# A quarter of the hypernetwork sums moves from TensorE's delta units to GpSimd

## The chip, the cores and the metric

The kernel runs on one core of a Trainium2 chip. The metric is the device time of one launch in microseconds. The five engines of the core run their own instruction streams and meet only at semaphores: TensorE (PE: matmuls, and transposes written as matmuls with an identity), VectorE (DVE), ScalarE (ACT), GpSimd (POOL), and SyncE (SP), which here issues the DMAs.

## The reference, cut to what matters

Two layers, one after the other, over x of shape 4 x 1024 x 512.

```python
# layer 0: a gated block with quantised down projection
scale = cond @ norm_w.T + 1.0
h = x * (scale[:, None, :] * rsqrt(mean(x * x) + EPS))
val, gate = split(h @ up_w.T, 2)             # 2 x 2048 columns
h = val * gelu(gate)
y = act_quant(h) @ weight_quant(down_w).T    # a scale for each row of h
x = y + x
# layer 1: an adapter whose weights depend on the batch
dWd = ((cond @ Wdd.T + bdd) * 0.1).reshape(B, 128, 512)   # Wdd: 65536 x 128
dWu = ((cond @ Wdu.T + bdu) * 0.1).reshape(B, 512, 128)   # Wdu: 65536 x 128
down = relu(einsum('bld,bnd->bln', x, Wd + dWd) + bd)
out = x + einsum('bln,bdn->bld', down, Wu + dWu) + bu
```

The change concerns `cond @ Wdd.T` and `cond @ Wdu.T`: four conditions of 128 numbers against 131,072 rows of 128 numbers, 64 MB of weights. They are called the deltas.

## The kernel before, in words

**Chunks and slots.** The 4096 rows of x are done in 8 chunks of 512 (`c` = 0 to 7). In each, layer 0 makes 16 tiles of h, one for each slot `j` (0 to 15) of the loop `run`. In slot j TensorE makes the gate product (12 matmuls of 512 columns into one of two GATE banks), then the value product (12 more into one of two VAL banks). ScalarE applies gelu to the gate; VectorE multiplies value, descale and gelu into h[j] (L925); ScalarE takes the absolute value of h[j] (L643), and VectorE, in the next slot, folds that into a running maximum (L839). After slot 15 the maximum is turned, gives a scale for each row, and in slots 0 to 7 of the next chunk VectorE multiplies the sixteen tiles of h by the scales (`quantise`, L812), with ScalarE rounding them. In slots 9 to 12 TensorE makes the down products of the chunk before, 16 matmuls each (`down_products`, L1188), and VectorE adds the residual one slot later (`residual`, L882).

**Waits that matter.** TensorE's gate product of slot n waits for gelu n-2, its value product for h n-2 (`pe.wait_ge(h_done, n - 1)`); a down product waits for the residual before it.

**Delta units.** The rows of Wdd and Wdu are cut into 128 units. For a unit SP loads two halves of 256 KB (`load_nat`, L352; a ring of three) and VectorE transposes each by 32 x 32 blocks (`turn_nat`, L829). After each eight units TensorE multiplies two batches of four units by the conditions (`delta_products`, L1147, 32 instructions for a batch, four column tiles of the array side by side). ScalarE copies the bank to `stage` (`read_sums`, L616), and SP stores it in DRAM (L356). The functions `units_at` and `batch_at` say in which slot that is.

**The end of the deltas.** In slot 6 of the last chunk SP reads all deltas back in the layout of the layers (`load_deltas`, L363 and L366). In slots 10 to 13 TensorE turns them, one batch of x a slot (`turn_deltas`, L1159 down, L1164 up), and in the following slot VectorE adds them to the base weights (`layer_of_batch`, L845 and L854). Then layer 1 runs over the eight chunks (the last 75 us).

**GpSimd** makes one small power for each chunk (`norm_x`, L509) and, at the end, adds bu to the rows (L534). Each engine carries out its program strictly in order; no scheduler is at work.

Of the kernel before, what the change touches and what calls it, by code (L numbers as in the profile page):

```python
# [15 lines left out]
P = 128  # L16
# [9 lines left out]
def conditioned_block(nc, x, cond, norm_w, up_w, down_w, Wd, bd, Wu, bu, Wdd, bdd, Wdu, bdu, out):  # L26
# [11 lines left out]
    GROUPS = 16  # L38
    UNITS, HALVES, NATT = 128, 3, 8
# [6 lines left out]
    delta_of = delta_dram.rearrange("g (t q b) (y k m) -> y b (g t) k q m", t=4, q=8, b=NB, y=2, k=2)  # L46
# [4 lines left out]
    with ExitStack() as ctx:  # L51
# [61 lines left out]
        with (nc.sbuf_tensor("delta_reg", [P, 2 * NATT + HALVES, 512], F32) as delta_reg,  # L113
              nc.sbuf_tensor("w_hi", [P, KD, 2 * FF], F16) as w_hi,
              nc.sbuf_tensor("w_lo", [P, KD, 2 * FF], F16) as w_lo):
            pass
# [15 lines left out]
        nat = delta_reg[:, 2 * NATT:, :]  # L132
# [11 lines left out]
        FIRST_SLOT, PAIRS = 3, 4  # L144

        def pieces(i):
            o = 2 * (FIRST_SLOT + i % PAIRS)
# [32 lines left out]
        def first_bank(c, k):  # L180
# [11 lines left out]
        nat_in = [sem(f"nat_in{t}") for t in range(HALVES)]  # L192
        upn_in = [sem(f"upn_in{i}") for i in range(3)]
# [17 lines left out]
        absrun_turned, max_read, scale_step, s_turned, s_bc_done = (sem(n) for n in (  # L211
            "absrun_turned", "max_read", "scale_step", "s_turned", "s_bc_done"))
# [69 lines left out]

        def units_at(c, j):
            if is_first(c):
                return [j - 13] if j >= 13 else []
            if c == NCH - 1:
                return [UNITS - 5 + j] if j < 5 else []
            u = 3 + 20 * (c - 1) + j + min(max(j - 9, 0), 4)
            return [u, u + 1] if 9 <= j < 13 else [u]

        def batch_at(c, j):
            before = units_at(c, j - 1) if j > 0 else units_at(c - 1, FT - 1) if c > 0 else []
            return [m for u in before if u % NATT == NATT - 1 for m in (u // 4 - 1, u // 4)]
# [7 lines left out]
        def _(sp):  # L301
# [44 lines left out]
            def load_nat(v):  # L346
                u, k = v // 2, v % 2
                m, t = u // 4, u % 4
                src = (Wdd, Wdu)[m % 2].rearrange("(a u p e) h -> u p a (e h)", a=2, p=P, e=4)[4 * (m // 2) + t, :, k, :]
# [8 lines left out]
            def load_deltas():  # L358
                sp.wait_ge(stage_free, 16 * (GROUPS + 1))
                sp.wait_ge(nat_turned, 2 * UNITS)  # L360
                for b in range(NB):
                    for k in range(2):
                        sp.dma_start(delta_d[64 * k:64 * k + 64, b, :], delta_of[0, b, :, k, 0:4, :]).then_inc(delta_back, 16)  # L363
                    for k in range(KD):
                        part = delta_of[1, b, 32 * (k % 2):32 * (k % 2) + 32, k // 2, 0:4, :]
# [1062 lines left out]
```

## Time and profile before

| | |
|---|---|
| time, median of 3 runs | 944.22 us (943.78 to 944.37) |
| time of the profiled execution | 944.56 us, its span 942.8 us |
| busy: PE, PEld, DVE, ACT, POOL | 934.1, 463.7, 675.2, 437.8, 53.3 us |
| granted TensorE clock | 0.999 of full speed |
| HBM | 112.72 MB read, 20.97 MB written |

Busy time is the time in which at least one instruction of the engine was under way. Matmuls are pipelined, so PE busy 99% of the span says that it was hardly ever without work, not that it worked at its peak. Times of the trace are counted from the span's start; what lies between the span and the execution's own time is 1.8 us.

### The profile page before, as it was taken

What the parts mean: (1) busy time and instruction counts of PE and PEld (TensorE: products, weight loads), DVE (VectorE), ACT (ScalarE), POOL (GpSimd) and SP (SyncE); (2) the same over time, 40 slices, a digit from 0 to 9 for tenths busy, and PEclk for the clock granted to TensorE, in tenths of its full rate; (3) what the DMA queues carried; (4) which work ended last, traced back from release to release, by engine and by line L of the source; (5) the groups of instructions that cost most, each with busy time, mean ns of one, the idle gap of its engine ahead of it and who ended that gap; (6) DMA issues with size and microseconds to landing.
All of it is one profiled execution on the core that took longest, in us unless ns stands there. A gap on an engine that the chain in (4) does not pass through costs nothing.

```text
span 942.8 us, 13789 instructions
## 1 busy us (share of the span) xinstructions
PE 934.1 (99%) x5266; PEld 463.7 (49%) x5266; DVE 675.2 (72%) x1030; ACT 437.8 (46%) x800; POOL 53.3 (6%) x53
## 2 busy tenths in 40 slices
PE   9999999999999999999999999999999999999998
PEld 6555544444444444444444444444444444445586
DVE  6778788767877596767877687767876684256766
ACT  7898677224731276214742166214642155114443
POOL 1000000000000000000000000000000000000564
PEclk9999999999999999999999999999999999999999
DMA  8899654564346543665347543555447434321584
GB/s 299 234 219 207 169 151 130 151 193 136 101 140 173 158 134 112 162 165 159 107 136 172 158 136 99 173 168 145 118 128 179 147 92 141 103 71 31 185 306 179
DMA packets 118810, 145.36 MB, mean 154 GB/s; under 512 B 51796, under 2 KB 57432, under 8 KB 118232
## 3 DMA queue, kind: packets, MB, share of 16 engines
q1 hardware_dynamic: 118744, 144.48, 53.7%
q8 instruction: 41, 0.67, 0.3%
q14 instruction: 25, 0.20, 0.1%
HBM read 112.72 MB, written 20.97 MB: 142 GB/s over the span
## 4 chain that ended last, share of the span: by engine, by line
PE 92%; DVE 3%; ACT 2%; issue 1%; DMA 1%; SPq 0%; POOL 0%; DVEq 0%; POOLq 0%; ACTq 0%
PE bank L1088 22%; PE bank L1089 22%; PE bank L1090 22%; PE bank L1188 10%; PE bank L1147 6%; PE bank L1198 1%; PE bank L1345 1%; PE bank L1323 1%; PE bank L1332 1%; DVE delta_reg L829 1%; PE bank L1068 1%; PE bank L1353 1%; PE bank L1355 1%; PE bank L1354 1%; PE bank L1362 1%
## 5 line engine op out<-in xcount | busy, mean ns | idle before, releaser
L1088 PE MATMUL bank<-x_split,w_hi 128*128 128x512 f16 x1016 | 385.3, 379 | 0.0
L1090 PE MATMUL bank<-x_split,w_lo 128*128 128x512 f16 x1016 | 385.2, 379 | 0.0
L1089 PE MATMUL bank<-x_split,w_hi 128*128 128x512 f16 x1016 | 385.2, 379 | 0.0
L829 DVE STREAM_TRANSPOSE delta_reg<-delta_reg 128x512 f32<-128x512 f32 x256 | 262.1, 1106 | 51.5 <-DMA delta_reg<-in_L_cond_Wdu 19.1
L643 ACT ACTIVATE g<-h 128x512 f32<-128x512 f32 x128 | 80.6, 630 | 304.8 <-DVE h L925 304.8
L1090 PEld LDWEIGHTS bank<-x_split,w_lo 128*128 128x128 f16 x1016 | 99.3, 98 | 119.8
L1088 PEld LDWEIGHTS bank<-x_split,w_hi 128*128 128x128 f16 x1016 | 99.4, 98 | 119.5 <-issue 6.6
L1089 PEld LDWEIGHTS bank<-x_split,w_hi 128*128 128x128 f16 x1016 | 99.4, 98 | 113.3
L925 DVE SCALAR_TENSOR_TENSOR h<-bank,desc,g 128x512 f32<-128x512 f32 x128 | 93.0, 727 | 83.6 <-issue 57.4
L627 ACT ACTIVATE g<-bank,desc 128x512 f32<-128x512 f32 x128 | 87.5, 684 | 115.8 <-PE bank L1090 115.3
L1188 PE MATMUL bank<-wqT,qreg 128*128 128x512 fp8e4 x448 | 101.3, 379 | 0.0
L839 DVE TENSOR_TENSOR absrun<-absrun,g 128x512 f32<-128x512 f32 x120 | 82.5, 687 | 24.5 <-ACT g L643 23.7
L812 DVE TENSOR_TENSOR h<-h,s_bc 128x512 f32<-128x512 f32 x112 | 71.7, 681 | 1.7 <-ACT s_bc L605 1.7
L1188 PEld LDWEIGHTS bank<-wqT,qreg 128*128 128x128 bf16 x448 | 43.8, 98 | 52.9
L598 ACT ACTIVATE h<-h 128x512 f32<-128x512 f32 x112 | 64.5, 622 | 9.2 <-DVE h L812 9.2
L601 ACT ACTIVATE qreg<-h 128x512 bf16<-128x512 f32 x112 | 63.6, 617 | 0.0
L1147 PE MATMUL bank<-delta_reg,cond_diag 128*32 128x256 f32 x1024 | 58.8, 381 | 0.1
L882 DVE SCALAR_TENSOR_TENSOR xr<-bank,fy,xr 128x512 f32<-128x512 f32 x30 | 22.4, 750 | 46.1 <-DMA xr<-in_x 20.3
L509 POOL TENSOR_TENSOR rstd<-ss,mhalf 128x4 f32<-128x4 f32 x7 | 9.7, 1379 | 666.0 <-DVE ss L776 666.0
L1147 PEld LDWEIGHTS bank<-delta_reg,cond_diag 128*32 128x32 f32 x1024 | 31.6, 110 | 26.4 <-issue 6.8
L573 ACT ACTIVATE xr<-qreg 128x512 f32<-128x512 f32 x32 | 20.1, 629 | 3.7 <-DMA qreg<-in_L_cond_up_w 3.1
L534 POOL TENSOR_TENSOR out_own<-xn,sc_row 128x512 f32<-128x512 f32 x8 | 10.0, 1288 | 195.8 <-DVE h L1032 193.3
(175 smaller groups left out, 628.0 us busy)
## 6 DMA issues: line engine op xcount, KB each, us to landing
delta_reg<-in_L_cond_Wdd SPq DMA_DIRECT2D x128, 256.0 KB, 2.9
delta_reg<-in_L_cond_Wdu SPq DMA_DIRECT2D x128, 256.0 KB, 2.9
qreg<-in_L_cond_up_w SPq DMA_DIRECT2D x32, 256.0 KB, 4.8
xr<-in_x SPq DMA_DIRECT2D x30, 256.0 KB, 3.7
x_scratch<-xr SPq DMA_DIRECT2D x30, 256.0 KB, 3.2
xn<-in_x SPq DMA_DIRECT2D x7, 1024.0 KB, 6.0
h<-in_L_cond_down_w SPq DMA_DIRECT2D x4, 1024.0 KB, 7.5
delta_reg<-in_L_cond_down_w SPq DMA_DIRECT2D x8, 512.0 KB, 4.8
```

The lines of the kernel that those rows point to most:

```text
L598: act.activation(h[:, k, :], h[:, k, :], ACT.Copy, bias=ROUND).then_inc(round_added, 1)
L627: act.activation(g[:, j % 2, :], GATE[j % 2][:, :], ACT.Gelu, scale=desc[:, 2 * j + 1:2 * j + 2]).then_inc(gelu_done, 1)
L643: act.activation(g[:, j % 2, :], h[:, j, :], ACT.Abs).then_inc(abs_done, 1)
L812: dve.tensor_tensor(h[:, k, :], h[:, k, :], s_bc[:, :], ALU.mult).then_inc(h_scaled, 1)
L829: dve.transpose(natT[:, t, k, :, :].rearrange("p a (r e) -> p e a r", e=4), nat[:, v % HALVES, :]).then_inc(nat_turned, 1)
L839: dve.tensor_tensor(absrun[:, :], absrun[:, :], g[:, j % 2, :], ALU.max).then_inc(max_done, 1)
L925: dve.scalar_tensor_tensor(h[:, j, :], VAL[j % 2][:, :], desc[:, 2 * j:2 * j + 1], g[:, j % 2, :], ALU.mult, ALU.mult).then_inc(h_done, 1)
L1088: pe.matmul(bank[:, :], w_hi[:, k, cols], xh[:, par, k, :], start=(k == 0), stop=False)
L1089: pe.matmul(bank[:, :], w_hi[:, k, cols], xl[:, par, k, :], start=False, stop=False)
L1090: mm = pe.matmul(bank[:, :], w_lo[:, k, cols], xh[:, par, k, :], start=False, stop=(k == KD - 1))
L1147: mm = pe.matmul(HY[32 * t:32 * t + 32, cols], cond_diag[:, a, :], natT[:, (4 * m + t) % NATT, :, a, :], start=(a == 0), stop=(a == HB - 1))
L1188: mm = pe.matmul(Y[:, :], q[:, f, t * P:(t + 1) * P], wqT[:, f, :], start=(f == 0), stop=(f == FT - 1))
```

## The change

- `UNITS` falls from 128 to 96: all of Wdd, and the half of Wdu that makes rows 0 to 127 and 256 to 383 of dWu. A batch is four units, `NATT` (the ring of transposed units) falls from 8 to 4, so that a batch must be multiplied before the next unit is transposed. A table `unit_slots` gives the slots, with one left out after each batch. TensorE's batches come singly.
- The other half of Wdu is 64 parts. For each, SP loads 256 KB as it lies (`load_part`, 512 runs of 512 bytes, a ring of three). GpSimd multiplies it by each of the four conditions (`multiply_part`: 4 products of 128x512), adds upper and lower half of the 128 columns (2 sums of 512 results), then again (2 sums of 256 results). VectorE sums the 32 that are left (`sum_part`, one reduction from 512 to 16 in each partition) and so has these columns of dWu in place without a turn. Parts have fixed slots in VectorE's order: 5, 7, 9, 10, 11, 12, 13, 15 of chunk 1; 1, 3, 5, 7, 9, 10, 11, 12, 13, 15 of chunks 2 to 6; 1, 3, 5, 7, 9, 10 of chunk 7.
- `s_bc` now holds the four conditions in all partitions, and VectorE's `quantise` reads the scales from the bank TB itself; ScalarE's copy of them is gone. `layer_of_batch` uses `stage` in place of `s_bc`.
- The turn of the up deltas is 2 transposes for a batch of x in place of 4, and stands behind the value product of its slot (`turn_delta_up`). The deltas come back by 32 DMAs in place of 24.

```diff
-    UNITS, HALVES, NATT = 128, 3, 8
+    UNITS, HALVES, NATT = 96, 3, 4
+    PARTS = 64
...
+        for n in range(FT * NCH):
+            long_slot = n >= FT and 9 <= n % FT < 13
+            while free_from <= n and sum(map(len, unit_slots.values())) < UNITS and len(unit_slots.get(n, [])) < 1 + long_slot:
+                u = sum(map(len, unit_slots.values()))
+                unit_slots.setdefault(n, []).append(u)
+                if u % NATT == NATT - 1:
+                    free_from = n + 2
...
+            def load_part(i):
+                if i >= 3:
+                    sp.wait_ge(part_step, 8 * (i - 3) + 6)
+                d = 128 + 4 * i + 128 * (i // 32)
+                sp.dma_start(part_w[:, i % 3, :, :], Wdu.rearrange("(d n) h -> n d h", n=BN)[:, d:d + 4, :]).then_inc(part_in[i % 3], 16)
...
+                    i = part_at(FT * c + j)
+                    if i is not None and 1 <= i < PARTS - 2:
+                        load_part(i + 2)
...
+            def multiply_part(i):
+                pool.wait_ge(part_in[i % 3], 16 * (i // 3 + 1))
+                for pair in range(2):
+                    if i > 0 or pair > 0:
+                        pool.wait_ge(part_step, 8 * i + 4 * pair)
+                    for b in range(2):
+                        pool.tensor_tensor(part_mul[:, b, :, :], part_w[:, i % 3, :, :],
+                                           cond_all[:, 2 * pair + b, :].unsqueeze(1).to_broadcast([P, 4, C]), ALU.mult).then_inc(part_step, 1)
+                    pool.wait_ge(part_step, 8 * i + 4 * pair + 2)
+                    pool.tensor_tensor(part_mul[:, :, :, 0:64], part_mul[:, :, :, 0:64], part_mul[:, :, :, 64:128], ALU.add).then_inc(part_step, 1)
+                    pool.wait_ge(part_step, 8 * i + 4 * pair + 3)
+                    if i > 0 and pair == 0:
+                        pool.wait_ge(part_summed, i)
+                    pool.tensor_tensor(part_low[:, 2 * pair:2 * pair + 2, :, :], part_mul[:, :, :, 0:32], part_mul[:, :, :, 32:64],
+                                       ALU.add).then_inc(part_step, 1)
...
-                    dve.wait_ge(s_bc_done, c + 1)
+                    dve.wait_ge(s_turned, c + 1)
...
-                    dve.tensor_tensor(h[:, k, :], h[:, k, :], s_bc[:, :], ALU.mult).then_inc(h_scaled, 1)
+                    dve.tensor_tensor(h[:, k, :], h[:, k, :], TB[:, :], ALU.mult).then_inc(h_scaled, 1)
...
+            def sum_part(i):
+                dve.wait_ge(part_step, 8 * i + 8)
+                dve.tensor_reduce(part_sum[:, :, 4 * i:4 * i + 4], part_low, AX.X, ALU.add).then_inc(part_summed, 1)
...
+            def turn_delta_up(b):
                 if b > 0:
                     pe.wait_ge(layers_ready, 2 * b)
-                for k in range(KD):
+                for k in range(0, KD, 2):
                     mm = pe.transpose(TB[:, k * P:(k + 1) * P], delta_u[:, k, b, :], identf[:, :])
                 mm.then_inc(delta_turned, 1)
```

Two places of the order show what moves. The first is SP's queue in slots 5 to 8 of the last chunk. Before, after the last loads of Wdu come the last store of `stage` (delta_scratch<-stage), the 24 loads of `load_deltas` (delta_reg<-delta_scratch), bu, and the residual's rows (xr<-in_x):

```order
L356 DMA delta_scratch<-stage 128x512
L363 DMA delta_reg<-delta_scratch 64x4x128 x2
L366 DMA delta_reg<-delta_scratch 128x1x128 x4
...
L363 DMA delta_reg<-delta_scratch 64x4x128 x2
L366 DMA delta_reg<-delta_scratch 128x1x128 x4
L446 DMA sc_row<-in_L_cond_bu 128x512
L371 DMA xr<-in_x 128x512 x2
```

Now L399 is `load_part`; the row of it above the store loads part 62, the one below bu loads part 63, the last:

```order
L399 DMA delta_reg<-in_L_cond_Wdu 128x4x128
L381 DMA delta_scratch<-stage 128x512
L389 DMA delta_reg<-delta_scratch 32x4x128
L392 DMA delta_reg<-delta_scratch 16x4x128 x2
L393 DMA delta_reg<-delta_scratch 128x1x128
...
L392 DMA delta_reg<-delta_scratch 16x4x128 x2
L393 DMA delta_reg<-delta_scratch 128x1x128
L488 DMA sc_row<-in_L_cond_bu 128x512
L399 DMA delta_reg<-in_L_cond_Wdu 128x4x128
L404 DMA xr<-in_x 128x512 x2
```

The load of part 63 stands behind the whole of `load_deltas`, eight groups of four DMAs.

The second place is VectorE in slots 9 to 11 of the last chunk. Before (L925 makes h, L839 is the running maximum, L882 the residual, L845 the first layer's weights):

```order
L925 SCALAR_TENSOR_TENSOR h<-bank,desc,g 128x512
L839 TENSOR_TENSOR absrun<-absrun,g 128x512
L882 SCALAR_TENSOR_TENSOR xr<-bank,fy,xr 128x512
L925 SCALAR_TENSOR_TENSOR h<-bank,desc,g 128x512
L839 TENSOR_TENSOR absrun<-absrun,g 128x512
L882 SCALAR_TENSOR_TENSOR xr<-bank,fy,xr 128x512
L845 SCALAR_TENSOR_TENSOR wd_first<-bank,base_wd 128x512
```

Now (L1006 makes h, L897 is the maximum, L960 the residual, L901 `sum_part`, L916 the first layer's down weights):

```order
L901 TENSOR_REDUCE delta_reg<-delta_reg 128x4x4
L1006 SCALAR_TENSOR_TENSOR h<-bank,desc,g 128x512
L897 TENSOR_TENSOR absrun<-absrun,g 128x512
L960 SCALAR_TENSOR_TENSOR xr<-bank,fy,xr 128x512
L901 TENSOR_REDUCE delta_reg<-delta_reg 128x4x4
L1006 SCALAR_TENSOR_TENSOR h<-bank,desc,g 128x512
L897 TENSOR_TENSOR absrun<-absrun,g 128x512
L960 SCALAR_TENSOR_TENSOR xr<-bank,fy,xr 128x512
L916 SCALAR_TENSOR_TENSOR wd_first<-bank,base_wd 128x512
```

The sum of a part stands ahead of the h of its slot; that of part 63 stands ahead of h of slot 10, the second residual and the first layer weights.

## Rows read from the trace of the kernel before

**Rows 1.** The page, parts 1 and 4: busy time, and the chain that ended last.

```profile
PE 934.1 (99%) x5266; PEld 463.7 (49%) x5266; DVE 675.2 (72%) x1030; ACT 437.8 (46%) x800; POOL 53.3 (6%) x53
...
PE 92%; DVE 3%; ACT 2%; issue 1%; DMA 1%; SPq 0%; POOL 0%; DVEq 0%; POOLq 0%; ACTq 0%
```

**Rows 2.** Groups by line, shapes apart: busy us, mean ns, idle before.

```profile
L829 DVE STREAM_TRANSPOSE delta_reg<-delta_reg 128x512 f32<-128x512 f32 x256 | 262.1, 1106 | 51.5 <-DMA delta_reg<-in_L_cond_Wdu 19.1 <-PE bank L1147 17.0 <-DMA delta_reg<-in_L_cond_Wdd 15.5
L812 DVE TENSOR_TENSOR h<-h,s_bc 128x512 f32<-128x512 f32 x112 | 71.7, 681 | 1.7 <-ACT s_bc L605 1.7
L1027 DVE TENSOR_TENSOR h<-bank,h 128x512 f32<-128x512 f32 x16 | 9.9, 681 | 0.0
L798 DVE TENSOR_REDUCE m<-bank 128x4 f32<-128x512 f32 x8 | 5.5, 690 | 5.8 <-PE bank L1172 5.8
```

**Rows 3.** Timeline of TensorE around two batches: start, us, instruction.

```profile
271.80 0.38 PE L1090 MATMUL bank<-x_split,w_lo 128*128 128x512 f16 x1
272.10 3.66 PE L1147 MATMUL bank<-delta_reg,cond_diag 128*32 128x256 f32 x64
275.70 0.39 PE L1088 MATMUL bank<-x_split,w_hi 128*128 128x512 f16 x1
275.92 0.38 PE L1089 MATMUL bank<-x_split,w_hi 128*128 128x512 f16 x1
```

**Rows 4.** Timeline of TensorE at the first turn, and a row of its waits.

```profile
817.41 0.60 PE L1159 MATMUL bank<-identf,delta_reg 128*128 128x128 f32 x4
817.84 0.60 PE L1164 MATMUL bank<-identf,delta_reg 128*128 128x128 f32 x4
...
PE bank L1164 <- DVE s_bc L854: 0.8, 2, 0.4
```

**Rows 5.** Timeline of GpSimd, three places.

```profile
1.32 0.29 POOL L500 TENSOR_SCALAR_AFFINE_SELECT identf<-identf 128x128 f32<-128x128 f32 x1 [0.24 <-POOL identb L497]
...
256.45 1.38 POOL L509 TENSOR_TENSOR rstd<-ss,mhalf 128x4 f32<-128x4 f32 x1 [104.02 <-DVE ss L776]
...
879.25 4.99 POOL L534 TENSOR_TENSOR out_own<-xn,sc_row 128x512 f32<-128x512 f32 x4 [193.32 <-DVE h L1032]
```

**Rows 6.** Timeline of VectorE while GpSimd's power at 256.45 runs.

```profile
256.20 0.17 DVE L776 TENSOR_SCALAR ss<-ss 128x4 f32<-128x4 f32 x1 [1.31 <-ACT x_split L546]
256.28 1.29 DVE L812 TENSOR_TENSOR h<-h,s_bc 128x512 f32<-128x512 f32 x2
257.48 0.68 DVE L839 TENSOR_TENSOR absrun<-absrun,g 128x512 f32<-128x512 f32 x1
```

**Rows 7.** Timeline: SP in chunk 1, VectorE's h in three slots.

```profile
139.56 9.11 SPq L352 DMA_DIRECT2D delta_reg<-in_L_cond_Wdd  x5
...
148.74 0.75 DVE L925 SCALAR_TENSOR_TENSOR h<-bank,desc,g 128x512 f32<-128x512 f32 x1 [0.42 <-issue]
...
744.89 0.75 DVE L925 SCALAR_TENSOR_TENSOR h<-bank,desc,g 128x512 f32<-128x512 f32 x1 [1.32 <-issue]
...
790.90 0.75 DVE L925 SCALAR_TENSOR_TENSOR h<-bank,desc,g 128x512 f32<-128x512 f32 x1 [6.33 <-issue]
```

**Rows 8.** Timeline of ScalarE and SP in slots 5 to 9 of the last chunk.

```profile
792.22 0.58 ACT L616 ACTIVATE stage<-bank 128x512 f32<-128x512 f32 x1
...
792.83 0.33 SPq L356 DMA_DIRECT2D delta_scratch<-stage  x1
794.85 1.35 SPq L363 DMA_DIRECT2D delta_reg<-delta_scratch  x2
796.24 2.55 SPq L366 DMA_DIRECT2D delta_reg<-delta_scratch  x4
...
811.38 0.59 SPq L446 DMA_DIRECT2D sc_row<-in_L_cond_bu  x1
```

**Rows 9.** DMA issues: median us to landing; the deltas' loads: minimum, median, maximum.

```profile
delta_reg<-in_L_cond_Wdu SPq DMA_DIRECT2D x128, 256.0 KB, 2.9
...
DMA to landing us min/median/max: 2.2/2.3/3.3
```

More of the change, by code:

```diff
@@ L111, in conditioned_block @@
         bdc = sb("bdc", [P, 1], F32)
-        with (nc.sbuf_tensor("delta_reg", [P, 2 * NATT + HALVES, 512], F32) as delta_reg,
+        with (nc.sbuf_tensor("delta_reg", [P, 19, 512], F32) as delta_reg,
               nc.sbuf_tensor("w_hi", [P, KD, 2 * FF], F16) as w_hi,
@@ L192, in conditioned_block @@
         nat_in = [sem(f"nat_in{t}") for t in range(HALVES)]
+        part_in = [sem(f"part_in{t}") for t in range(3)]
+        cond_all_in, part_step, part_summed, layers_wide = sem("cond_all_in"), sem("part_step"), sem("part_summed"), sem("layers_wide")
         upn_in = [sem(f"upn_in{i}") for i in range(3)]
@@ L347, in load_nat @@
                 u, k = v // 2, v % 2
-                m, t = u // 4, u % 4
-                src = (Wdd, Wdu)[m % 2].rearrange("(a u p e) h -> u p a (e h)", a=2, p=P, e=4)[4 * (m // 2) + t, :, k, :]
+                layer, four = batch_of(u // 4)
+                src = (Wdd, Wdu)[layer].rearrange("(a u p e) h -> u p a (e h)", a=2, p=P, e=4)[4 * four + u % 4, :, k, :]
                 if v >= HALVES:
@@ L432, in run @@
                                 load_nat(v)
+                    if c == 1 and j == 3:
+                        sp.wait_ge(piece_quant, FT)
+                        for i in range(3):
+                            load_part(i)
+                    i = part_at(FT * c + j)
+                    if i is not None and 1 <= i < PARTS - 2:
+                        load_part(i + 2)
                     if not first:
@@ L509, in norm_x @@
                 pool.tensor_tensor(rstd[:, :], ss[:, :], mhalf[:, :], ALU.pow).then_inc(x_rstd, 1)
-            def run(c, par, b):
-                if b is not None:
-                    norm_x(c + 1)
+            def multiply_part(i):
[13 more added lines that the diff above has]
+                                       ALU.add).then_inc(part_step, 1)
+            def run(c, par, b):
+                if is_first(c):
+                    norm_x(1)
+                    pool.wait_ge(cond_all_in, 16)
+                for j in range(FT):
+                    if j == 9 and c > 0 and b is not None:
+                        norm_x(c + 1)
+                    i = part_at(FT * c + j)
+                    if i is not None:
+                        multiply_part(i)
             for i in range(2):
@@ L634, in run @@
                         w_square(j + 3)
-                    if not first and j == 0:
-                        copy_scales(c - 1)
                     if not first and j < 8:
@@ L905, in run @@
                         turn_units(c, j)
+                    i = part_at(n)
+                    if i is not None:
+                        sum_part(i)
                     if last and 11 <= j < 15:
@@ L1246, in run @@
                         pe.matmul(TA[:, 0:1], ones[:, :], wtot[:, 0:1], start=True, stop=True).then_inc(ta_full, 1)
+                    if last and 10 <= j < 14:
+                        turn_delta_up(j - 10)
                     if not first and j == 0:
```

100 lines of the change are left out of this document (62 added, 38 removed).

## The prediction

> **What bounds the kernel now.** I read the page first: TensorE is busy for 99% of the span, and 92% of the chain that ended last is TensorE's own [rows 1]. So an instruction taken from TensorE's stream is worth its pitch in that stream, and whatever else the change does is worth nothing until TensorE waits for it. Next I read the timelines slot by slot. In this text a slot is 24 matmuls at the pitch 275.92 - 275.70 = 0.22 us (0.216 over longer stretches) [rows 3], thus 5.18 us, and 16 x 0.216 = 3.45 us more where a down product stands. GpSimd has almost nothing to do: a power of 1.38 us for each chunk until the adds at the end [rows 5]. That idle engine gets 64 parts of work, and VectorE, in the middle of its own order, waits for each. So I read what GpSimd's instructions cost, and then the queue of SP in the last chunk, where the deltas come back.
>
> **What TensorE saves.** A pair of batches lies between 271.80 and 275.70, where otherwise one pitch would lie: 3.90 - 0.22 = 3.68 us [rows 3]. There are 16 pairs: 58.9 us. Of a pair, 63 pitches fill 3.66 - 0.38 = 3.28 us, 0.052 each; the rest, 0.40 us, is getting into and out of the narrow tiles and is paid at each visit. A single batch thus costs 31 x 0.052 + 0.40 = 2.02 us (bounds: half a pair, 1.84, and 2.1), and 24 of them cost 48.5 us. Saved: 10.4 us (8.5 to 14.7). The up turns are 2 transposes in place of 4: a group of 4 takes 817.84 - 817.41 = 0.43 us, so 4 x 0.22 = 0.9 us. TensorE's waits at the up turn, 0.8 us [rows 4], are covered by the value product that now stands ahead. Together 12.1 us, which alone would make 944.6 - 12.1 = 932.5 us. (The sum is made against the profiled execution's 944.56 us, 0.3 us over the median.)
>
> **What VectorE and ScalarE trade.** VectorE loses 64 transposes of about 1.1 us and gains 64 reductions like L798's 0.69 us [rows 2]: 26 us less. Reading the scales from the bank costs nothing: the same product with one operand in a bank also takes 681 ns [rows 2]. ScalarE loses copies. None of this is on TensorE's path; the cover is VectorE's 28% of idle time, and if that cover went, the reductions (44 us) would be the most that it could cost. The loads move the same bytes in runs of 512 bytes; such a load has three parts' time to land, against 2.9 us now [rows 9], so I cost it at nothing (bound: with less than one part, about 10 us, it stays nothing).
>
> **What a part costs GpSimd.** Four adds of 128x512 take 4.99 us [rows 5]: start to start 1.24 us, one alone about 1.29. A sum of 256 results I put at 0.70 (bounds 0.62 and 0.87). An instruction that waits for one of GpSimd's own starts 0.24 us after its end (L500) [rows 5]; the bounds of this step are 0.08, what lies between the end of VectorE's L776, 256.37, and the power at 256.45 [rows 5, 6], and 0.25. A pair of conditions is: product, product, wait, sum, wait, sum, wait: 1.24 + 1.29 + 1.29 + 0.70 + 3 x 0.25 = 5.27 us. A part is twice that, **10.5 us** (bounds 9.3 and 11.0), and each chunk adds a power, 1.6 us with its wait.
>
> **What VectorE grants.** Ten parts and a power need 107 us; a chunk has 16 x 5.18 + 4 x 3.45 + 4 x 2.02 + 1, some 106 us. So it is close, and must be counted along the line. SP reaches the first part's load after VectorE's unit of slot 3, where it now stands at 139.56 [rows 7]; 1.7 us earlier with one batch fewer by then; landed at 141. The hardest place is slot 13 of chunk 6, after a run of five parts in slots 8.6 us apart. Before, its h starts at 744.89 [rows 7]; 14 pairs (51.5 us) between slot 5 of chunk 1 and there become 21 batches (42.4 us), so with the 1.7 it is due at 734.1. It needs part 56, the 57th: 141 + 57 x 10.54 + 6 x 1.6 = 751.4. That is 17 us late. TensorE bears about 6 us of lateness on VectorE (the residual in the next slot must be there before the next down product, and the h product one and a half slots on). GpSimd then costs 17 - 6 = **11 us**. This term turns on the part: each 0.1 us of it is 5.7 us, and below 10.35 us it is nothing. With 11.0 it is 38 us.
>
> **What the end of the deltas costs.** The last batch now stands in slot 6 of the last chunk, not 5. Count from the end of value product 6. As now (h at 790.90, copy 792.22, store 792.83, first load 794.85) [rows 7, 8] the copy, the store and the first load follow at +1.4, +2.0 and +4.0. 24 loads took SP 811.38 - 794.85 = 16.5 us, 0.69 each, in groups of four 0.65, whether of 64 or 128 KB [rows 8]. 32 of them at 0.65 take 20.8 us (18 to 22): issued by +24.8, landed by +27 [rows 9]. TensorE wants them after slots 7, 8, 9, a down product and a gate product, at 3 x 5.18 + 3.45 + 2.6 = +21.6: a wait of 5 us at the first down turn, where today 3.7 us are to spare. Worse, the load of part 63 is queued behind all of it and bu's 0.6: issued +25.4, landed +28.5, multiplied +39, reduced +39.7; then h of slot 10, its absolute value, the maximum, the residual and the first layer's down weights, 3.5 us: +43.2. TensorE stands at the second down turn from +27 + 3.3 + 3.45 + 2.6 = +36.3: another 7 us. Together **12 us**, and with VectorE some 5 us late as above, the copy to `stage` is as late: 17 us.
>
> **Sum of the forecast.** 944.6 - 12.1 + 11 + 17 = 960.5; I say **961 us**. Its own range is 947 to 1000 (a part of 10.35 to 11.0 and some sharing, below).
>
> **The rivals.**
>
> *The port is blocked* (24%). VectorE's instructions with two operands in SBUF (15 maxima, 4 scalings, 4 differences a chunk, 0.68 us each) might keep GpSimd from reading for their whole length: 23 x 0.68 / 10 = 1.56 us more for each part, 12.1 in all. Then 57 x 1.56 = 89 us come on top, and 5 us more at the end: 961 + 94 = 1055 us; half as much sharing gives about 1005. For it: nothing in the trace, since GpSimd's adds at the end lie beside products with a bank. Against it: the power at 256.45 lies over L812 and L839, which both have two operands in SBUF, and they run at 0.64 and 0.68 us as elsewhere [rows 5, 6]; but it reads only four numbers. The Trainium skill ("SBUF — State Buffer", section "Who interferes with whom") says that such an instruction contends with a GpSimd instruction that reads SBUF, and that the one that comes second is blocked for the whole instruction. On the rows of the power the trace does not agree with a lock of that length; for long reads no run here shows it yet.
>
> *GpSimd keeps pace, the end takes the gain back* (19%). A part under 10.35 us, for instance 9.9 with waits of 0.14: the 11 us go, VectorE is on time, and 944.6 - 12.1 + 12 = 944 us, no change to be measured.
>
> *Faster* (17%). GpSimd keeps pace, and SP issues the loads of 32 KB faster, as it does a plain load (0.33 for L356) [rows 8]: 16 of them at 0.33 take 5 us off both waits: 944 - 5 = 939 us. It decides as soon as the last wait falls below 10 us; it ends at 932.5 if both were covered.
>
> **How the numbers follow.** 40% for the forecast (947 to 1000), 24% for the port, 19% and 17% for the two others. The predicted time is 961. A range from 940 to 1045 leaves out half of the last case and a part of the port's. What a measurement of this kernel tells from no change is about 0.2%, 1.9 us: 942.3 to 946.1. Faster: 17% and a fifth of the third case, 21%. Same: 11%. Slower: 68%.
>
> **What the profile after would show.** TensorE: single batches of 2.0 us, and a total of about 48 us for them. GpSimd: product groups of 2.5 us and part to part 10.5 us without a gap for VectorE's wait; busy for some 600 us. VectorE: `sum_part` waiting for GpSimd in slots 10 to 13 of each chunk, with TensorE then waiting for h or the residual. The port would show in products over 1.4 us beside maxima or maxima over 0.8 us. The end: SP in `load_deltas` for 21 us, TensorE waiting 5 us or more at the down turn of slot 10, and again at slot 11 for the weights that stand behind part 63. I would be wrong if GpSimd's own waits are cheap, if VectorE's port matters, or if SP's small loads are.

## The result and the profile after

| | before | after |
|---|---|---|
| time, median | 944.07 us (943.78 to 944.37) | 981.38 us (978.99 to 985.78) |
| ratio, 95% interval | | 1.040 (1.039 to 1.042) |
| span of the profiled execution | 942.8 us | 976.9 us |

The changed kernel is 37 us slower. The forecast was 961 us, so its sign and its range (940 to 1045) held, and its size did not: it saw +17 us. The page of the changed kernel, parts 1 and 4, answers to [rows 1]:

```profile
PE 931.7 (95%) x5002; PEld 453.9 (46%) x5002; DVE 736.2 (75%) x1034; ACT 427.3 (44%) x788; POOL 682.4 (70%) x565
...
PE 11%; ACT 1%; issue 0%; DVE 0%; DVEq 0%
```

TensorE did 264 instructions fewer and still left 45 us of the span idle, against 9 before. VectorE is busier by 61 us, where the forecast saw it 26 us less busy. (The chain breaks off after 12% of the span and says nothing here.) The groups by line, shapes apart, of GpSimd and VectorE in the changed kernel, which answer to [rows 2]:

```profile
L559 POOL TENSOR_TENSOR delta_reg<-delta_reg,s_bc 128x512 f32<-128x512 f32 x256 | 354.3, 1405 | 120.4 <-DMA delta_reg<-in_L_cond_Wdu 106.8 <-POOL delta_reg L566 0.9
L562 POOL TENSOR_TENSOR delta_reg<-delta_reg 128x512 f32<-128x512 f32 x128 | 178.4, 1394 | 10.0
L897 DVE TENSOR_TENSOR absrun<-absrun,g 128x512 f32<-128x512 f32 x120 | 129.5, 1079 | 24.3 <-ACT g L702 23.7
L566 POOL TENSOR_TENSOR delta_reg<-delta_reg 128x256 f32<-128x256 f32 x128 | 98.9, 772 | 39.0 <-DVE delta_reg L901 29.8
L870 DVE TENSOR_TENSOR h<-h,bank 128x512 f32<-128x512 f32 x112 | 71.3, 677 | 0.0
L901 DVE TENSOR_REDUCE delta_reg<-delta_reg 128x16 f32<-128x512 f32 x64 | 42.2, 659 | 56.0 <-POOL delta_reg L566 55.9
L852 DVE TENSOR_TENSOR xn<-xn,xn_hi 128x512 f16<-128x512 f32 x28 | 38.8, 1384 | 0.0
L847 DVE SCALAR_TENSOR_TENSOR xn<-xn,rstd,sc_row 128x512 f32<-128x512 f32 x28 | 25.9, 924 | 0.0
L863 DVE TENSOR_SCALAR fy<-mc,wtot 128x4 f32<-128x4 f32 x8 | 8.3, 1037 | 0.0
```

The same groups of the kernel before:

```profile
L839 DVE TENSOR_TENSOR absrun<-absrun,g 128x512 f32<-128x512 f32 x120 | 82.5, 687 | 24.5 <-ACT g L643 23.7
L794 DVE TENSOR_TENSOR xn<-xn,xn_hi 128x512 f16<-128x512 f32 x28 | 19.0, 678 | 0.0
L805 DVE TENSOR_SCALAR fy<-mc,wtot 128x4 f32<-128x4 f32 x8 | 1.8, 224 | 0.0
```

The maxima rose from 687 to 1079 ns, the differences from 678 to 1384, the scalings (L847) from 731 to 924, a small fy from 224 to 1037 ns: 47 + 20 + 5 + 7 = 79 us more on VectorE. Those with one operand in a bank did not move (L870, 677 ns). The waits of the changed kernel, by engine, line and what was waited for: us in total, times, longest.

```profile
PE bank L1228 <- DVE delta_reg L887: 12.0, 8, 2.4
PE bank L1257 <- DVE absrun L897: 11.3, 5, 3.1
PE bank L1273 <- DVE xr L960: 8.7, 6, 3.0
...
DVE delta_reg L901 <- POOL delta_reg L566: 55.9, 20, 8.0
```

TensorE waits for VectorE at three kinds of place: the batches (a unit is transposed late), the turn of the maximum, and the down product behind a late residual. VectorE waits for GpSimd, and GpSimd for VectorE (29.8 us, in the group L566 above). The timeline of GpSimd in the last chunk, where VectorE stands still, gives a part without a neighbour:

```profile
847.98 2.48 POOL L559 TENSOR_TENSOR delta_reg<-delta_reg,s_bc 128x512 f32<-128x512 f32 x2 [15.31 <-DMA delta_reg<-in_L_cond_Wdu]
850.54 1.26 POOL L562 TENSOR_TENSOR delta_reg<-delta_reg 128x512 f32<-128x512 f32 x1
851.88 0.72 POOL L566 TENSOR_TENSOR delta_reg<-delta_reg 128x256 f32<-128x256 f32 x1
...
856.59 0.72 POOL L566 TENSOR_TENSOR delta_reg<-delta_reg 128x256 f32<-128x256 f32 x1
```

From 847.98 to 857.31 it takes 9.3 us, and GpSimd goes on 0.08 us after its own result, not 0.25. In the middle of the kernel a part is longer: the three groups make 631.6 us for 64 parts, 9.87, and with the same 0.4 us of gaps 10.3 us. What happens there shows in the timelines of GpSimd and of VectorE in one slot of chunk 2:

```profile
289.79 3.28 POOL L559 TENSOR_TENSOR delta_reg<-delta_reg,s_bc 128x512 f32<-128x512 f32 x2
...
290.18 1.75 DVE L852 TENSOR_TENSOR xn<-xn,xn_hi 128x512 f16<-128x512 f32 x1
291.86 1.75 DVE L897 TENSOR_TENSOR absrun<-absrun,g 128x512 f32<-128x512 f32 x1
```

Two products take 3.28 us instead of 2.48, and L852 and L897 take 1.75 us each instead of 0.68. I read this as each of VectorE's two waiting for the end of the product under way, and the next product for its end. The Trainium skill ("SBUF — State Buffer", section "Who interferes with whom") has this as an exclusive lock between a VectorE instruction with two SBUF inputs and a GpSimd instruction that reads. On these rows the trace agrees: an instruction of 0.68 us that becomes one of 1.75 has waited 1.07 us, nearly a whole product of 1.25.

The end of the deltas, as the timelines of the changed kernel show it (SP's first load, the loads of bu and of part 63; TensorE's down products of slots 9 and 10 and its down turns):

```profile
824.53 0.34 SPq L389 DMA_DIRECT2D delta_reg<-delta_scratch  x1
...
842.39 0.59 SPq L488 DMA_DIRECT2D sc_row<-in_L_cond_bu  x1
843.03 0.43 SPq L399 DMA_DIRECT2D delta_reg<-in_L_cond_Wdu  x1
843.50 0.98 SPq L404 DMA_DIRECT2D xr<-in_x  x2
...
835.86 3.62 PE L1273 MATMUL bank<-wqT,qreg 128*128 128x512 fp8e4 x16
843.96 0.66 PE L1240 MATMUL bank<-identf,delta_reg 128*128 128x128 f32 x4 [1.90 <-DMA delta_reg<-delta_scratch]
849.44 5.31 PE L1273 MATMUL bank<-wqT,qreg 128*128 128x512 fp8e4 x16 [2.02 <-DVE xr L960]
861.39 1.11 PE L1240 MATMUL bank<-identf,delta_reg 128*128 128x128 f32 x4 [4.04 <-DVE wd_first L916]
```

SP needs 842.39 - 824.53 = 17.9 us for the 32 loads. Part 63 and the rows of the residual come behind them; TensorE waits three times, as the last three rows show.

**Where the 34 us of span are.** Two marks cut the program: VectorE's `ss` of chunk 6 (L834), and h of slots 9 and 11 of the last chunk.

```profile
706.64 1.20 DVE L834 TENSOR_SCALAR ss<-ss 128x4 f32<-128x4 f32 x1 [1.31 <-ACT x_split L611]
...
836.11 0.75 DVE L1006 SCALAR_TENSOR_TENSOR h<-bank,desc,g 128x512 f32<-128x512 f32 x1 [2.30 <-issue]
...
866.18 0.75 DVE L1006 SCALAR_TENSOR_TENSOR h<-bank,desc,g 128x512 f32<-128x512 f32 x1 [4.18 <-issue]
```

Before, the same instructions stand here:

```profile
684.30 0.17 DVE L776 TENSOR_SCALAR ss<-ss 128x4 f32<-128x4 f32 x1 [1.31 <-ACT x_split L546]
...
811.62 0.75 DVE L925 SCALAR_TENSOR_TENSOR h<-bank,desc,g 128x512 f32<-128x512 f32 x1 [3.04 <-PE bank L1090]
...
830.64 0.75 DVE L925 SCALAR_TENSOR_TENSOR h<-bank,desc,g 128x512 f32<-128x512 f32 x1 [4.17 <-issue]
```

Up to h of slot 9 the change costs 836.11 - 811.62 = 24.5 us, although TensorE has some 10 us less to do there. From slot 9 to slot 11 it costs 30.1 - 19.0 = 11.1 us. Behind that it gives back 1.4 us. So the middle went wrong; the end cost 11 us, where the forecast had 12 and 5 more with VectorE late.

**TensorE's clock has a share in it.** Behind five of TensorE's waits, of 2.0 to 4.0 us, the granted clock reads 0.50 of full speed in windows of 1 us, the level of 1.2 GHz. The first two on TensorE's timeline, and the window of the first (us, busy time of PE, PEld, DVE, ACT and POOL, granted clock, DMA share, GB/s):

```profile
202.47 5.15 PE L1273 MATMUL bank<-wqT,qreg 128*128 128x512 fp8e4 x16 [2.98 <-DVE xr L960]
662.46 3.20 PE L1228 MATMUL bank<-delta_reg,cond_diag 128*32 128x256 f32 x32 [2.09 <-DVE delta_reg L887]
...
202.00:206.00 4.00, 3.53 (x10) 1.34 (x11) 3.33 (x5) 0.00 (x0) 3.70 (x5) 0.57 0.37 102
```

Sixteen down matmuls took 5.15 us in place of 3.62, and a batch 3.20 in place of 1.93. By the windows each such stretch costs (1 - 0.57) x 4 = 1.7 us. Two lie ahead of `ss` of chunk 6, the third ahead of h of slot 9, two behind it: an estimated 8.5 of the 34 us are clock, and they come from the waits. The kernel before has no such stretch until its last 2 us.

### The profile page after: what moved, and what is told of

It reads as the page before. It is cut to its first block and busy times, and to the rows that moved or that the text cites. A ratio compares the mean times of both kernels' runs of the same rounds, so it can differ in the third digit from the quotient of the medians.

```text
span 976.9 us, 13872 instructions
## 1 busy us (share of the span) xinstructions
PE 931.7 (95%) x5002; PEld 453.9 (46%) x5002; DVE 736.2 (75%) x1034; ACT 427.3 (44%) x788; POOL 682.4 (70%) x565
## 5 line engine op out<-in xcount | busy, mean ns | idle before, releaser
L559 POOL TENSOR_TENSOR delta_reg<-delta_reg,s_bc 128x512 f32<-128x512 f32 x256 | 354.3, 1405 | 120.4 <-DMA delta_reg<-in_L_cond_Wdu 106.8
L887 DVE STREAM_TRANSPOSE delta_reg<-delta_reg 128x512 f32<-128x512 f32 x192 | 197.3, 1106 | 15.6 <-DMA delta_reg<-in_L_cond_Wdd 11.5
L562 POOL TENSOR_TENSOR delta_reg<-delta_reg 128x512 f32<-128x512 f32 x128 | 178.4, 1394 | 10.0
L897 DVE TENSOR_TENSOR absrun<-absrun,g 128x512 f32<-128x512 f32 x120 | 129.5, 1079 | 24.3 <-ACT g L702 23.7
L1006 DVE SCALAR_TENSOR_TENSOR h<-bank,desc,g 128x512 f32<-128x512 f32 x128 | 94.0, 734 | 53.7 <-issue 34.9
L566 POOL TENSOR_TENSOR delta_reg<-delta_reg 128x256 f32<-128x256 f32 x128 | 98.9, 772 | 39.0 <-DVE delta_reg L901 29.8
L1273 PE MATMUL bank<-wqT,qreg 128*128 128x512 fp8e4 x448 | 104.5, 388 | 8.9 <-DVE xr L960 8.7
L901 DVE TENSOR_REDUCE delta_reg<-delta_reg 128x16 f32<-128x512 f32 x64 | 42.2, 659 | 56.0 <-POOL delta_reg L566 55.9
L870 DVE TENSOR_TENSOR h<-h,bank 128x512 f32<-128x512 f32 x112 | 71.3, 677 | 0.0
L1228 PE MATMUL bank<-delta_reg,cond_diag 128*32 128x256 f32 x768 | 47.7, 390 | 12.0 <-DVE delta_reg L887 12.0
```

Source lines behind the costliest of these rows:

```text
L559: pool.tensor_tensor(part_mul[:, b, :, :], part_w[:, i % 3, :, :], cond_all[:, 2 * pair + b, :].unsqueeze(1).to_broadcast([P, 4, C]), ALU. ...
L562: pool.tensor_tensor(part_mul[:, :, :, 0:64], part_mul[:, :, :, 0:64], part_mul[:, :, :, 64:128], ALU.add).then_inc(part_step, 1)
L566: pool.tensor_tensor(part_low[:, 2 * pair:2 * pair + 2, :, :], part_mul[:, :, :, 0:32], part_mul[:, :, :, 32:64], ALU.add).then_inc(part_s ...
L887: dve.transpose(natT[:, t, k, :, :].rearrange("p a (r e) -> p e a r", e=4), nat[:, v % HALVES, :]).then_inc(nat_turned, 1)
L897: dve.tensor_tensor(absrun[:, :], absrun[:, :], g[:, j % 2, :], ALU.max).then_inc(max_done, 1)
L1006: dve.scalar_tensor_tensor(h[:, j, :], VAL[j % 2][:, :], desc[:, 2 * j:2 * j + 1], g[:, j % 2, :], ALU.mult, ALU.mult).then_inc(h_done, 1)
```

## The experiments

| kernel | time, us | ratio to before | `ss` of chunk 6 |
|---|---|---|---|
| before | 944.07 | | 684.30 |
| after | 981.38 | 1.040 (1.039 to 1.042) | 706.64 |
| part63_first | 972.77 | 1.030 (1.028 to 1.033) | |
| sum_free | 948.20 | 1.005 (1.003 to 1.007) | 684.15 |
| write_only | 962.73 | 1.020 (1.018 to 1.021) | 692.62 |
| pool_tiny | 934.99 | 0.991 (0.989 to 0.992) | 675.26 |
| write_only_fast | 947.48 | 1.004 (1.002 to 1.005) | 679.04 |
| tail_full | 969.44 | 1.027 (1.026 to 1.029) | |
| half_sums | 973.09 | 1.031 (1.029 to 1.033) | 702.25 |
| half_tail | 961.22 | 1.019 (1.017 to 1.021) | |
| half_duty | 935.45 | 0.991 (0.990 to 0.992) | 679.59 |
| upturn_alone | 942.60 | 0.999 (0.998 to 1.000) | |
| ahead | 964.60 | 1.023 (1.019 to 1.026) | 694.65 |
| ahead_tail | 952.26 | 1.009 (1.007 to 1.010) | 695.71 |

Edits are against the changed kernel unless another is named.

**pool_tiny**: what is left when GpSimd does nearly nothing.

```diff
-                        pool.tensor_tensor(part_mul[:, b, :, :], part_w[:, i % 3, :, :],
-                                           cond_all[:, 2 * pair + b, :].unsqueeze(1).to_broadcast([P, 4, C]), ALU.mult).then_inc(part_step, 1)
+                        pool.tensor_tensor(part_mul[:, b, :, 0:2], part_w[:, i % 3, :, 0:2],
+                                           cond_all[:, 2 * pair + b, 0:2].unsqueeze(1).to_broadcast([P, 4, 2]), ALU.mult).then_inc(part_step, 1)
```

(and both sums likewise on one or two columns)

> The same instructions and waits on GpSimd, each on 2 to 8 elements in each partition (the sums of the parts are left out of the result). Neither pace nor port is left, and part 63 needs 1 to 2 us in place of 9.3. Both theories: 940 to 944 us, of which about 5 us is SP's tail. If it stays above 955 something else in the change costs: the single batches, the new order of units, or the loads in runs of 512 bytes.

935 us. Here h of slot 9 of the last chunk starts at 799.37, 12.25 us before the 811.62 of the kernel before: the saving on TensorE is real. A batch by itself, on TensorE's timeline of this kernel, the products on each side of it:

```profile
259.81 0.38 PE L1171 MATMUL bank<-x_split,w_lo 128*128 128x512 f16 x1
260.12 1.93 PE L1228 MATMUL bank<-delta_reg,cond_diag 128*32 128x256 f32 x32
261.98 0.39 PE L1169 MATMUL bank<-x_split,w_hi 128*128 128x512 f16 x1
```

261.98 - 259.81 - 0.22 = 1.95 us, where the forecast had 2.02. This kernel is the floor for the others: `ss` at 675.26. It keeps the loads in runs of 512 bytes, the single batches and the new order of units, so none of these costs what the changed kernel loses.

**sum_free**: GpSimd does all its work, and VectorE's reductions read other data, so VectorE waits for GpSimd only once, before the first layer's weights. The sums of the parts are left out of the result.

```diff
-                dve.wait_ge(part_step, 8 * i + 8)
-                dve.tensor_reduce(part_sum[:, :, 4 * i:4 * i + 4], part_low, AX.X, ALU.add).then_inc(part_summed, 1)
+                dve.tensor_reduce(part_sum[:, :, 4 * i:4 * i + 4],
+                                  identf[:, :].rearrange("p (d h) -> p d h", d=4).unsqueeze(1).to_broadcast([P, NB, 4, 32]),
+                                  AX.X, ALU.add).then_inc(part_summed, 1)
```

> VectorE's 64 reductions read the identity and wait for nothing; GpSimd does all its work as before (the sums of the parts are left out of the result). VectorE waits for GpSimd once, at the first layer's weights. Theory of pace (chunks 1 to 6 are longer because VectorE waits for the parts, 56 us in all): the 31 us of the middle go, 950 to 953 us. Theory of the port (VectorE is late because its own instructions with two operands in SBUF, and its small ones, wait for GpSimd's reads): VectorE's maxima stay at 1.0 to 1.1 us and the time stays above 970.

948 us. The port alone, without the waits between the two engines, costs 684.15 - 675.26 = 8.9 us by the mark, though VectorE's maxima are as long as in the changed kernel (groups of this kernel; the differences took 1342 ns):

```profile
L897 DVE TENSOR_TENSOR absrun<-absrun,g 128x512 f32<-128x512 f32 x120 | 128.0, 1066 | 24.0 <-ACT g L702 23.7
```

**write_only**: GpSimd fills memory and reads nothing, at 10.3 us a part; VectorE waits for it as before. The products and sums are left out; `fill_twice` makes two memsets, of 1024 and of 256 columns.

```diff
-                    for b in range(2):
-                        pool.tensor_tensor(part_mul[:, b, :, :], part_w[:, i % 3, :, :],
-                                           cond_all[:, 2 * pair + b, :].unsqueeze(1).to_broadcast([P, 4, C]), ALU.mult).then_inc(part_step, 1)
+                    for k in range(3):
+                        fill_twice(n + k, 1024, 256)
```

> GpSimd's products and sums are replaced by fills that read nothing and take as long as a part took under load, 10.4 us (the sums of the parts are left out of the result); VectorE waits for them as before. Pace: the same 975 to 981 us. Port: VectorE's maxima fall back from 1079 to about 690 ns, TensorE's waits in the middle mostly go, and the time is 950 to 960 us.

963 us. The maxima are back to what they take before (groups of this kernel; the differences took 685 ns), and VectorE's wait for GpSimd is 74.6 us:

```profile
L900 DVE TENSOR_TENSOR absrun<-absrun,g 128x512 f32<-128x512 f32 x120 | 82.6, 688 | 24.5 <-ACT g L705 23.7
L904 DVE TENSOR_REDUCE delta_reg<-delta_reg 128x16 f32<-128x512 f32 x64 | 42.7, 668 | 74.7 <-POOL delta_reg L560 74.6
```

The pace alone costs 17.4 us by the mark, of which an estimated 5.1 us is slow clock behind TensorE's waits (the granted clock is 0.58 from 202 to 206 us and 0.57 from 229 to 237; sum_free and pool_tiny have no such stretch ahead of the mark, the changed kernel 3.4 us). Pace and port one by one make 26.3 us; together, in the changed kernel, they cost 31.4.

**write_only_fast**: the same with the second fill of each pair cut from 256 to 96 columns, a part of 9.5 us.

> As write_only (fills that read nothing; the sums of the parts are left out of the result), but a part takes 9.5 us in place of 10.3, close to what the real instructions take alone (9.3). If the pace of GpSimd costs only because the port stretches a part from 9.3 to over 10, the middle is back at its floor and the time is 943 to 947 us (935 of the run with tiny instructions, and 9 at the end for a part of full length). Rival: the run of five parts in slots 8.6 us apart makes VectorE late at any part above 8.6: 953 to 960.

947 us; by the mark 3.8 us over the floor. So 0.8 us of a part is worth 13.6 us up to there, 5.1 of them the slow clock, which this kernel does not have ahead of the mark. The pace is a cliff, and 10.3 us lies behind it.

**part63_first** and **tail_full**: the order of SP's queue in the last chunk. The first loads part 63 ahead of the deltas. The second also moves the residual's rows ahead of them and gives each batch of x its own semaphore.

```diff
+                    if last and j == 6:
+                        load_part(PARTS - 1)
...
-                        if j in (7, 8):
+                        if j in (7, 8) and not last:
+                        if last and j == 6:
+                            load_xr(c - 1, 0)
+                            load_xr(c - 1, 1)
```

> One edit: the load of part 63 is issued ahead of the 32 loads of the deltas. The changed kernel takes 981.4 us. If the tail of SP's queue costs what its profile shows at slots 10 and 11 of the last chunk (11 us between the h products of slots 9 and 11, of which VectorE's wait for GpSimd is 8.0), this gives 974 to 976 us: what is left is the landing of the deltas (1.9) and the residual's rows, still behind them. Rival: the residual's rows, which land 10.4 us late for VectorE, set the same end, and the time stays within 2 us of 981.

> The changed kernel with SP's end put in another order: part 63 and the two rows of the residual ahead of the deltas' loads, and a semaphore for each batch of x, so that TensorE waits for 8 loads in slot 10 and not for 32. The load of part 63 alone gave 972.8. If the rest of the tail (1.9 us at the first turn, about 1 at the residual) is real, 968 to 971; if the late VectorE sets that end, 973.

972.8 and 969.4 us. Part 63 alone is worth 8.6 us: h of slots 9 and 11 are 21.3 us apart (837.02 and 858.33), against 30.1. The clock shares in that: the changed kernel has two slow stretches there, an estimated 3.4 us, and part63_first none. The residual's rows and the wait of the first turn are 3.3 us more.

**half_sums** and **half_tail**: GpSimd halves the products once, not twice, and VectorE's reduction reads 64 columns in place of 32; then the same with the order of the loads, where only the residual's rows go ahead of the deltas and the deltas one slot later, behind part 63. Both have a ring of two loads in place of three.

```diff
-                    pool.tensor_tensor(part_mul[:, :, :, 0:64], part_mul[:, :, :, 0:64], part_mul[:, :, :, 64:128], ALU.add)
-                    pool.tensor_tensor(part_low[:, 2 * pair:2 * pair + 2, :, :], part_mul[:, :, :, 0:32], part_mul[:, :, :, 32:64],
+                    pool.tensor_tensor(part_low[:, 2 * pair:2 * pair + 2, :, :], part_mul[:, :, :, 0:64], part_mul[:, :, :, 64:128],
```

> GpSimd halves the products once and VectorE sums 64 numbers in place of 32 (a load ring of two). A part alone takes about 7.9 us in place of 9.3, VectorE's reduction 1.2 in place of 0.66 us: 34 us more for VectorE, 90 us less for GpSimd. If pace and port together cost the middle 37 us: VectorE no longer waits for parts, the port's share (13 us with its tail, in the run where VectorE waits for nothing) shrinks with GpSimd's busy time, 945 to 955 us. Rival: VectorE, longer by 34 us of reductions and with more lateness from the port, becomes what TensorE waits for: 965 or more.

> half_sums with the order of the end as in tail_full (the deltas' loads in slot 7, behind part 63 and the residual's rows, and a semaphore for each batch of x). The end should give 8 to 11 us back: 936 to 946 us, under the kernel before if half_sums is at 953 or less.

973 and 961 us. My theory of that moment, that a shorter part on GpSimd is all that is needed, fell. VectorE waits only 15.8 us for GpSimd now, and TensorE still waits 14.2 us for residuals (waits of half_sums), because VectorE has 64 reductions of 1184 ns and, with the port, maxima of 1172:

```profile
PE bank L1271 <- DVE xr L958: 14.2, 10, 2.4
...
L899 DVE TENSOR_REDUCE delta_reg<-delta_reg 128x16 f32<-128x1024 f32 x64 | 75.8, 1184 | 15.8 <-POOL delta_reg L564 15.8
```

VectorE's reserve, which the forecast took as cover, is as small as GpSimd's.

**half_duty**: tail_full with every second part on two columns only.

> This is tail_full with every second part multiplied on two of its 128 columns only (the same instructions and waits, 0.1 to 0.3 us each), so that GpSimd does half of the work and has some 10 us of slack behind each whole part. Rows 64 parts wide are otherwise as in the changed kernel; half of the sums are left out. My theory: the middle costs more than port and pace by themselves because they meet (9.6 us for the port alone, 20.7 for the pace alone, 36.7 together). With half of the reading the port alone should cost about 4.8 us over the 935 us of the kernel with tiny parts, the pace nothing, and the order of loads should give back a few us: 936 to 942 us, VectorE's maxima at 0.8 to 0.9 us on average, and next to no wait of VectorE for GpSimd. Rival: the loss goes with the amount of GpSimd's reading alone, whatever the slack: half of the 34 us between tail_full (969) and tiny parts (935) is then left, about 952 us.

935 us. Up to the mark half of the reading costs 4.3 us, half of sum_free's 8.9; behind the mark it needs 3.9 us less than pool_tiny (253.5 against 257.4), with the other order of loads and an estimated 1.9 us less of slow clock. With slack behind each part the port is cheap.

**ahead** and **ahead_tail**: two buffers for what GpSimd leaves, so that it may end part i + 1 before VectorE has summed part i (the ring of loads falls to two for the room); then with the order of the loads, part 63 behind the deltas of batch 0.

```diff
-        part_low = delta_reg[:, 16, :].rearrange("p (b d h) -> p b d h", b=NB, d=4)
+        part_low = delta_reg[:, 15:17, :].rearrange("p s (b d h) -> p s b d h", b=NB, d=4)
...
-                    if i > 0 and pair == 0:
-                        pool.wait_ge(part_summed, i)
+                    if i > 1 and pair == 0:
+                        pool.wait_ge(part_summed, i - 1)
```

> The changed kernel with two buffers for the 32 results that GpSimd leaves, so that it may end part i + 1 before VectorE has summed part i; the ring of loads falls from three to two for the room. In the changed kernel a chunk of the middle takes 110.4 us (VectorE's ss from 154.55 to 706.64 is five chunks), and GpSimd fills it: ten parts at 10.3 us, the power, and some 5 us of waiting for VectorE's sum. Theory: GpSimd's chain sets the chunk, and it can't store up time in the slots where parts stand 10.4 us apart for the slots 9 to 13 where they stand 8.6 apart, because it may lead by less than half a part. Then most of the 5 us a chunk comes back: 950 to 965 us, and GpSimd's waits for VectorE (29.8 us) shrink below 10. Rival: VectorE's own instructions, stretched by the port, are what is late; GpSimd then only waits elsewhere, and the time stays within 975 to 985 us.

> The same two buffers together with the other order of SP's queue in the last chunk (residual rows ahead of the deltas, part 63 behind the deltas of batch 0 of x, a semaphore for each batch of x). All of the changed kernel's work is done. By the first theory 940 to 955 us, the best form of this change so far; by the rival about that of the kernel with the order alone, 969 us. Whether any form of the full change falls below the 944 us of before is open; I expect that it does not.

964.6 and 952.3 us. The rival falls: GpSimd's 29.8 us of waiting for VectorE are gone from the list of waits, VectorE's waits for GpSimd fall from 55.9 to 37.5 us, and TensorE's three kinds of waits fall by 44 to 65% (waits of ahead). GpSimd waits 24 us more for loads instead (130.4 against 106.8 us), since its ring is shorter.

```profile
PE bank L1228 <- DVE delta_reg L887: 5.5, 5, 2.0
PE bank L1273 <- DVE xr L960: 4.9, 3, 2.6
PE bank L1257 <- DVE absrun L897: 4.0, 3, 2.0
...
DVE delta_reg L901 <- POOL delta_reg L566: 37.5, 14, 8.0
```

The `ss` of chunk 1, five chunks ahead of the mark, in the changed kernel and in ahead:

```profile
154.55 0.17 DVE L834 TENSOR_SCALAR ss<-ss 128x4 f32<-128x4 f32 x1 [1.31 <-ACT x_split L611]
```

```profile
155.96 0.17 DVE L834 TENSOR_SCALAR ss<-ss 128x4 f32<-128x4 f32 x1 [1.31 <-ACT x_split L611]
```

A chunk takes (706.64 - 154.55) / 5 = 110.4 us in the changed kernel and (694.65 - 155.96) / 5 = 107.7 in ahead; in pool_tiny 105.1 (from 149.75 to 675.26). ahead_tail does all of the changed kernel's work in 29 us less, and is still 0.9% slower than before.

**upturn_alone**: the kernel before, with the up turn behind the value product and nothing else.

```diff
+            def turn_delta_up(b):
                 if b > 0:
                     pe.wait_ge(layers_ready, 2 * b)
...
                     up_products(par, j, VAL[j % 2], val_full)
+                    if last and 10 <= j < 14:
+                        turn_delta_up(j - 10)
```

> The kernel before with one edit of the change alone: the four transposes of the up deltas stand behind the value product of their slot. The forecast put TensorE's waits there at 0.8 us and the slots 12 and 13 of the changed kernel were 0.85 us shorter each, of which 0.22 us are the two transposes that went. If the turn's place is worth what those slots show, the kernel takes 1.5 to 2.5 us less than before, 941.5 to 942.5 us. Rival: the gain comes back at the maximum's turn behind slot 15, which waits for the layers, and the time is that of before, 944 us.

942.6 us. TensorE's waits at L1164 [rows 4] are gone. It is the one version that does all the work and is faster than the kernel before, by 0.14% (0.05 to 0.23%).

## Why the prediction was right or wrong

**TensorE saves 12.1 us: right in kind, 2 us too little.** The forecast had 10.4 us for the batches; pool_tiny shows 12.25 up to slot 9, mostly since a single batch takes 1.95 us and not 2.02. The up turns come on top, with the 1.7 us that the forecast gave them: slots 12 and 13 take 9.29 us in place of 10.14.

**GpSimd costs 11 us: this step failed, and with it the sum.** The middle, up to h of slot 9, costs 24.5 + 12.25 = 36.7 us over the floor; an estimated 5.1 of these are slow clock behind three of TensorE's waits, for which the forecast had no term. Three things in this step were wrong.

1. "None of this is on TensorE's path; the cover is VectorE's 28% of idle time." The port was weighed as a rival that lengthens only GpSimd's parts, and VectorE's instructions stayed at their price of before. The runs show it on both sides: a part goes from 9.3 to 10.3 us, and VectorE has 79 us more to do. The idle 28% are not where VectorE is late. write_only takes the reading away and keeps the pace at 10.3 us: the maxima fall from 1079 to 688 ns, and by the mark 14 us come back (706.64 to 692.62).
2. "Below 10.35 us it is nothing." The forecast looked for the hardest place and named slot 13 of chunk 6. By its own numbers slot 13 of chunk 1 is already bad: the seventh part is ready at 141 + 7 x 10.35 + 1.6 = 215.1 and is due at 147.0 + 8 x 5.18 + 4 x 3.45 + 2 x 2.02 = 206.3, 8.8 us late, of which 6 were said to be borne. VectorE waits for the very first part:

```profile
151.90 0.69 DVE L901 TENSOR_REDUCE delta_reg<-delta_reg 128x16 f32<-128x512 f32 x1 [4.72 <-POOL delta_reg L566]
```

With 10.3 us and no port the middle costs 17 us up to the mark (write_only), with 9.5 us 3.8.

3. "141 + 57 x 10.54" lets GpSimd run without ever waiting for VectorE. With one buffer of results it may lead by two products and a sum, 3.8 of 10.3 us, and the run of five parts 8.6 us apart needs 4 x (10.3 - 8.6) = 6.8 us of lead. So it idles ahead of the dense slots and is late in them. Ten parts of 10.3, 1.2 for the power and 5 us of waiting for VectorE (29.8 over six chunks) make 109 of the chunk's 110.4 us. ahead shows it: without that wait a chunk is 2.7 us shorter, 12 us up to the mark and 17 us in the end.

That the part was put at 10.5 us and measured 10.3 is an accident: its own waits were put at 0.25 us and take 0.08, and the port made up for it. The two errors met because the rivals "the port is blocked" and "GpSimd keeps pace" were kept apart. sum_free and write_only each undo one of them, and cost 8.9 and 17.4 us; half_duty, with half of the parts' work, ends within 0.5 us of the floor.

**The end costs 17 us: the queue right, the size 11 us.** "The load of part 63 is queued behind all of it" is worth 8.6 us by itself (part63_first). TensorE's three waits there make 1.9 + 2.0 + 4.0 = 7.9 us, against 12 in the forecast; that 11 came out is luck in part, for an estimated 3.4 us are the clock behind the second and the third. SP's 32 loads took 17.9 us and not 20.8, so the wait at the first down turn was 1.9 us and not 5. In its place came a wait that the forecast had not seen, though its order showed it: the residual's rows stand in the same queue, and the second down product waited 2.0 us for them. The 5 us more "with VectorE late" did not come: when VectorE is late, TensorE is too, and that is already paid in the middle.

**Reading the scales from the bank costs nothing: right** (L870, 677 ns, [rows 2] 681).

**The port's rival.** Its mechanism was right and its size too large: "23 x 0.68 / 10 = 1.56 us more for each part" measured 1.0, and it left out the 79 us on VectorE's side. It was given 24%, since the power of [rows 5, 6] ran beside two such instructions that kept their length. That row was a bad witness: it read four numbers, where the products read 512. The 1055 us of that rival did not come: a part without the port takes 9.3 us and not 10.5, so that with the port it is 10.3 and not 12.1.

**Open.** How pace and port share the 31.4 us up to the mark can't be told to the last 5 us, since each run that undoes one of them also shifts when VectorE and GpSimd meet, and which of TensorE's waits the slow clock follows. A kernel that gives GpSimd an eighth of the sums was not built; half_duty's 935.5 us and four more batches at 1.95 make about 943 us for it (an estimate), which is no gain over the 944 of before.

## What to carry to other kernels

An engine that was idle is not free: ask first which operand reads it shares with the engine beside it, and price the sharing on both engines, in the slots where work is due, not against an average of idle time. When a producer and a consumer run at nearly the same pace, count how far the one may lead (the buffers between them) against how dense the deadlines get; a pace that suffices on average costs its shortfall in every dense stretch. And when a load joins an in-order queue, list everything that now stands behind it, and put first what is waited for first. Where TensorE waits at all, look at its granted clock behind the wait: here that added an estimated 8.5 us.

## What the runs showed of the hardware that was not expected

- A small instruction can be lengthened by as much as a large one. fy, a TENSOR_SCALAR on 128x4, took 1037 ns on average beside GpSimd's products, against 224 before and 355 in sum_free. Reads alone do not explain it: beside fills it took 533 ns on average in write_only and 767 in write_only_fast. What it waits for is not shown.
- For the large two-operand instructions fills are no such neighbour: beside GpSimd's memsets they kept 688 and 685 ns. So the Trainium skill says it too ("SBUF — State Buffer", section "Who interferes with whom").
- GpSimd starts an instruction 0.08 us after the end of its own that it waits for (850.46 to 850.54, above), though the row of L500 in [rows 5] showed 0.24.
- TensorE's clock is not always full behind a wait. The windows of the changed kernel behind the second wait of the end (columns as above):

```profile
848.00:852.00 4.00, 2.56 (x9) 1.04 (x10) 0.75 (x1) 0.00 (x0) 3.84 (x4) 0.84 0.20 77
852.00:856.00 4.00, 4.00 (x15) 1.62 (x14) 0.00 (x0) 0.00 (x0) 3.84 (x4) 0.73 0.00 0
```

The value ahead of the last two is the granted clock, 0.84 and 0.73 of full speed: part of these stretches ran at the level of 1.2 GHz, the rest at 2.4. The sixteen matmuls at 849.44 took 5.31 us in place of 3.62: a wait of 2.0 us cost 3.7. Not every wait has this behind it: after the 1.90 us ahead of 843.96 the products ran at full pace (granted clock 1.00 from 842 to 848 us).
